# Transposing the rows of the experts and the logits by SyncE's DMAs in place of TensorE

## The reference

```python
xn = (xf - mu) * rsqrt(var + LN_EPS) * ln_scale + ln_bias
logits = xn @ gate_w.T                                   # 8 experts
tk_probs, tk_idx = top_k(softmax(logits), 2)
out = _swiglu(xf, sWg, sWu, sWd)                         # the shared expert, all rows
for e in range(NUM_EXPERTS):
    out = out + w[:, e:e + 1] * _swiglu(xf, Wg[e], Wu[e], Wd[e])
# _swiglu(x, wg, wu, wd) = silu(x @ wg) * (x @ wu) @ wd; 256 -> 512 -> 256
```

## Time and profile before

| what | us |
|---|---|
| median of 3 runs | 1809.16 |
| lowest and highest of the 3 | 1805.05, 1817.86 |
| the profiled execution | 1808.69 |
| its span, which the profile shows | 1807.0 |

### The profile page before, as it was taken

One profiled execution on the slowest core, in us unless ns is written; L12 is line 12 of the kernel. 1 busy time (PEld: TensorE's weight loads), 2 busy tenths in 40 slices (PEclk: granted clock), 3 DMA queues, 4 the chain that ended last, 5 costly groups with the idle time before them and its releaser, 6 DMA issues.

```text
span 1807.0 us, 44792 instructions
## 1 busy us (share of the span) xinstructions
PE 1611.0 (89%) x15824; PEld 1177.5 (65%) x15827; DVE 1105.0 (61%) x1938; ACT 881.9 (49%) x1305; POOL 888.4 (49%) x1125
## 2 busy tenths in 40 slices
PE   2589999999999999766987859979999999999996
PEld 2345555555555555356866737768999999999985
DVE  6568888888888888753764735653444444444432
ACT  1366676676666666543422325633444444444442
POOL 1145555555555555312034445625666666666652
PEclk9799999999999999986999979989999999999999
DMA  2323333333333333235366213222434334343432
GB/s 67 97 92 97 107 111 110 108 109 107 110 108 107 118 106 95 81 110 162 114 187 176 85 39 88 77 83 48 65 64 64 64 61 67 60 65 61 65 59 25
DMA packets 162574, 163.52 MB, mean 90 GB/s; under 512 B 23537, under 2 KB 153073, under 8 KB 162418
## 3 DMA queue, kind: packets, MB, share of 16 engines
q1 hardware_dynamic: 132210, 125.65, 22.7%
q0 software_dynamic: 30208, 35.81, 12.8%
HBM read 100.82 MB, written 60.30 MB: 89 GB/s over the span
## 4 chain that ended last, share of the span: by engine, by line
PE 67%; DMA 8%; issue 7%; DVE 6%; SPq 4%; ACT 3%; POOL 2%; another core or an unknown queue 2%; DVEq 0%; POOLq 0%; ACTq 0%
PE bank L1571 19%; PE pair_s L1861 13%; PE bank L1704 7%; PE pair_t L1861 6%; PE bank L1861 6%; PE pair_s L1631 4%; PE pair_t L1678 3%; PE bank L1739 3%; PE pair_t L1849 2%; SPq L435 2%; DMA wbuf<-in_L_ffn_Wu 2%; ACT prob L861 2%; DMA qk_d<-qkl 1%; DMA x_in<-xhl_d 1%
## 5 line engine op out<-in xcount | busy, mean ns | idle before, releaser
L861 ACT ACTIVATE prob<-pair_t 128x1024 f32<-128x1024 f32 x320 | 327.4, 1023 | 230.2 <-PE pair_t L1678 225.3
L665 POOL TENSOR_SCALAR_AFFINE_SELECT prob<-prob 128x256 f32<-128x256 f32 (+1 forms) x448 | 199.1, 458 | 324.6 <-ACT prob L861 320.2
L789 POOL DMA_INDIRECT out_x<-ysb,tok_rows x136 | 218.4, 1606 | 204.1 <-ACT ysb L1004 158.2
L968 ACT CAST early<-early 128x512 f16<-128x512 f32 (+1 forms) x208 | 125.1, 602 | 298.7 <-DVE early L1484 244.7
L1484 DVE SCALAR_TENSOR_TENSOR early<-pair_s,h_s,sg 128x512 f32<-128x512 f32 (+1 forms) x104 | 75.9, 729 | 243.6 <-PE pair_s L1861 209.6
L1490 DVE TENSOR_TENSOR early<-early 128x512 f16<-128x512 f32 (+1 forms) x208 | 139.2, 669 | 119.7 <-ACT early L968 86.7
L752 POOL DMA_INDIRECT tok_d<-tok_w,dest_i x128 | 130.3, 1018 | 157.6 <-PE bank L1861 69.0
L1861 PE MATMUL pair_s<-xt,wbuf 128*128 128x256 f16 (+1 forms) x1728 | 197.3, 270 | 4.5 <-DVE xt L1535 3.6
L1571 PE MATMUL bank<-wbuf,early 128*128 x1632 | 190.4, 273 | 0.9 <-ACT ysb L1004 0.8
L1704 PE MATMUL bank<-prob,v_op 128*32 128x512 f32 (+3 forms) x2048 | 181.2, 449 | 5.3 <-POOL prob L665 5.2
L1861 PEld LDWEIGHTS pair_s<-xt,wbuf 128*128 x1728 | 164.8, 99 | 26.6 <-issue 5.2
(11 more groups left out here) (261 smaller groups left out, 3051.9 us busy)
## 6 DMA issues: line engine op xcount, KB each, us to landing
q_op<-qk_d SPq DMA_DIRECT2D x192, 64.0 KB, 2.4
k_op<-qk_d SPq DMA_DIRECT2D x192, 64.0 KB, 2.4
x_in<-in_L_attn_x SPq DMA_DIRECT2D x16, 512.0 KB, 4.1
qk_d<-qkh SPq DMA_DIRECT2D x32, 256.0 KB, 2.2
qk_d<-qkl SPq DMA_DIRECT2D x32, 256.0 KB, 2.4
xres<-in_L_attn_x SPq DMA_DIRECT2D x16, 512.0 KB, 4.4
x_d<-x SPq DMA_DIRECT2D x32, 256.0 KB, 2.1
xhl_d<-xhl SPq DMA_DIRECT2D x32, 256.0 KB, 2.5
```

Of the source, the lines that this page charges most:

```text
L665: last = nc.gpsimd.affine_select(out=v, in_=v, compare_op=ALU.is_ge, fill=0.0, base=0, pattern=[[0, v.shape[1]], [1, P]], channel_multipli ...
L789: pool.indirect_dma_start(out=out, out_offset=bass.IndirectOffsetOnAxis(ap=tok_rows[:, k, 0:1], axis=0), in_=ysb[:, k % ROWS_AHEAD], in_of ...
L861: nc.scalar.activation(prob[:, half, u].rearrange("p a n -> p (a n)"), pair_t[:].rearrange("p a n -> p (a n)"), ACT.Exp, scale=exp_by).the ...
```

## The change

Every transpose of `xhl_d` rows, 8 (or 4) blocks of 128x128 per unit and 8 per logit pair, leaves PE, and with it the copy out of PSUM on ACT or VectorE. SyncE issues transposing DMAs (`dma_start_transpose`) instead, which write columns straight to SBUF:

- logits: one DMA of 512 rows per quad from DRAM, three buffers (two over `x_in`, one over `xn`) in place of two;
- shared expert: one DMA of 256 rows per unit from DRAM into `xts`, four buffers that lie over `xrow`; PE reads them there, and `xt2` is not used;
- routed stage: POOL gathers to `xrow` as before, and SP transposes each block, 128 rows, from `xrow` to `xt2`, SBUF to SBUF.

Waits follow: `columns(u)` waits for the hidden products of unit u-4, `gathered_columns` for those of unit u-2 and for the gather, PE for the transposes, `gather` for the transposes of the block eight before. The first four blocks' transposes stand in SP's program ahead of the last two stores of the shared stage.

```diff
-            def logit_rows(q):
-                if q < 2:
+            def logit_columns(q):
+                if q == 0:
                     sp.wait_ge(S["xn_done"], NB)
                     sp.wait_ge(S["stats_taken"], NB)
-                else:
-                    sp.wait_ge(S["lxT_in"], 2 * q - 2)
+                elif q == 2:
+                    sp.wait_ge(S["xnT_in"], 2 * NB)
+                elif q > 2:
+                    sp.wait_ge(S["lg_in"], 2 * (q - 3) + 2)
                 for j in range(2):
                     sp.wait_ge(xhl_stored[j], 16 * (q + 1))
-                sp.dma_start(lrow[:, q % 2], xhl_d[4 * P * q:4 * P * (q + 1), :].rearrange("(t p) n -> p t n", p=P)
-                             ).then_inc(lrow_loaded[q % 2], 16)
+                sp.dma_start_transpose(xtl[q % 3], xhl_d[4 * P * q:4 * P * (q + 1), :]).then_inc(xtl_loaded[q % 3], 16)
...
-            def rows(n):
-                if n >= GATHERED:
-                    sp.wait_ge(S["xT_in"], n - GATHERED + 1)
-                sp.dma_start(xrow[:, n % GATHERED], xhl_d[n * P:(n + 1) * P, :]
-                             ).then_inc(row_loaded[n % GATHERED], 16)
+            def columns(u):
+                if u >= 4:
+                    sp.wait_ge(S["u_in"], 2 * (u - 4) + 2)
+                sp.dma_start_transpose(xts[:, u % 4], xhl_d[2 * P * u:2 * P * (u + 1), :]).then_inc(xts_loaded[u % 4], 16)
...
+            def gathered_columns(k):
+                u, t = (k // 2, k % 2) if k < 2 * DBL else (k - DBL, 0)
+                if u > 1 and t == 0:
+                    sp.wait_ge(S["u_in"], 2 * (u + SH_UNITS - 2) + 2)
+                sp.wait_ge(row_gathered[k % GATHERED], 16 * (k // GATHERED) + 16)
+                sp.dma_start_transpose(xt2[:, u % 2, :, P * t:P * (t + 1)], xrow[:, k % GATHERED]
+                                       ).then_inc(xtr_loaded[u % 2], 16)
+
             for u in range(SH_UNITS):
+                if u == SH_UNITS - 1:
+                    for k in range(4):
+                        gathered_columns(k)
                 if u == LOADS_AT:
                     sp.wait_ge(S["lg_in"], TILES // 2)
+                if u + 4 < SH_UNITS:
+                    columns(u + 4)
                 for n in (2 * u, 2 * u + 1):
-                    if n + 6 < TILES:
-                        rows(n + 6)
                     store(n)
...
+            for k in range(4, BLOCKS):
+                gathered_columns(k)
...
             def gather(k):
-                pool.wait_ge(S["xT_in"], N_SH + k - GATHERED + 1)
+                if k < GATHERED:
+                    pool.wait_ge(S["u_in"], 2 * (SH_UNITS - 4 + k // 2) + 2)
+                else:
+                    done = k - GATHERED
+                    u = done // 2
+                    pool.wait_ge(xtr_loaded[u % 2], 32 * (u // 2) + 32)
...
             def routed(u, first, slot, turn, sizes):
                 par, (before, n, after) = slot_parity(u, slot), sizes
                 begin = at(offset[par])
+                pe.wait_ge(xtr_loaded[par], arrived(u, slot, turn))
                 for hh in range(2):
-                    unit_hidden(u + SH_UNITS, par, hh, P * n, begin)
+                    unit_hidden(u + SH_UNITS, xt2[:, par], hh, P * n, begin)
...
-                    unit_rows(u + (SH_UNITS + 1), row_gathered, [place_of(slot, turn, n + t) for t in range(after)])
```

More of the change, by code:

```diff
@@ L176, in build @@
         xhl = sb_a("xhl", [P, 2, 2, 2, C], F16)
-        lrow = x_in[:].rearrange("p a t c -> p (a t c)").bitcast(F16).rearrange("p (a t n) -> p a t n", a=2, t=4)
-        xtl = xn[:].rearrange("p t c -> p (t c)").bitcast(F16).rearrange("p (a t c n) -> p a t c n", a=2, t=2, c=2 * CC)
+        xtl = [x_in[:, k].rearrange("p t c -> p (t c)").bitcast(F16).rearrange("p (c n) -> p c n", c=2 * CC)
+               for k in range(2)]
+        xtl.append(xn[:].rearrange("p t c -> p (t c)").bitcast(F16).rearrange("p (c n) -> p c n", c=2 * CC))
         ctx_a.close()
@@ L194, in build @@
         spare = wbuf[:, (E - 1) * SLOT:]
[L195 to L197 removed]
+        xtl_end = spare[:, 0:2 * CC * 4 * P].rearrange("p (c n) -> p c n", c=2 * CC)
+        xts = xrow[:].rearrange("p g n -> p (g n)").rearrange("p (a c n) -> p a c n", a=4, c=2 * CC)
         zero_h = sb("zero_h", [P, 2 * C], F16)
@@ L239, in build @@
         ps_x16 = ps_x[:].bitcast(F16)
-        ps_lx = [bank[k][:].bitcast(F16) for k in (0, 1, 4, 6)]
         ps_r = bank[5]
@@ L336, in batches @@
             body(NB + 1, 1, cur=False, prev=False, prev2=True, nxt=False, nxt2=False)
-        row_loaded = [S[f"row_in{k}"] for k in range(GATHERED)]
+        xtr_loaded = [S[f"xtr_in{k}"] for k in range(2)]
+        xts_loaded = [S[f"xts_in{k}"] for k in range(4)]
         row_gathered = [S[f"rowg{k}"] for k in range(GATHERED)]
@@ L343, in build @@
         scattered = [S[f"scattered{k}"] for k in range(3)]
-        lrow_loaded = [S[f"lrow_in{k}"] for k in range(3)]
+        xtl_loaded = [S[f"lrow_in{k}"] for k in range(4)]
         N_SH = TILES
@@ L555, in load_matrix @@
                 sp.dma_start(dst.rearrange("p (c n) -> p c n", n=w.shape[2]), w).then_inc(S["w_exp"], 16)
-            for n in range(2):
-                rows(n)
-            sp.dma_start(lrow_end, xhl_d[NTOK - 4 * P:NTOK, :].rearrange("(t p) n -> p t n", p=P)
-                         ).then_inc(lrow_loaded[2], 16)
-            for n in range(2, 6):
-                rows(n)
+            columns(0)
+            sp.dma_start_transpose(xtl_end, xhl_d[NTOK - 4 * P:NTOK, :]).then_inc(xtl_loaded[3], 16)
+            for u in range(1, 4):
+                columns(u)
             for n in range(ROWS_AHEAD):
@@ L1543, in routed @@
                 unit_hidden(u + SH_UNITS, 1, P * n, 0)
-                if after:
-                    unit_rows(u + 1, 1 - par, first + (n + after), P * after)
                 unit_low(u + SH_UNITS, par, 1, P * n)
-            unit_rows(0, 0, 2, 2 * P)
             routed_units(dve, routed)
@@ L1789, in body, with logits @@
                         if k < PAIRS:
[L1790 to L1812 removed]
+                            logits(k, xtl[k // 2 % 3], xtl_loaded[k // 2 % 3], 16 * (k // 6) + 16)
+            def logits(k, columns, loaded, arrived):
+                pe.wait_ge(loaded, arrived)
                 if k == 0:
@@ L1839, in at, with hidden_half @@
                 return pe.snap(register, min_val=0, max_val=(E - 1) * SLOT)
-            def unit_rows(u, arrived, places):
-                for t, (here, count) in enumerate(places):
-                    pe.wait_ge(arrived[here], count)
-                    if t == 0 and some(u):
-                        pe.wait_ge(S["xt_done"], u)
-                    for c in range(2 * CC):
-                        to = P * (len(places) * c + t)
-                        last = nc.tensor.transpose(ps_x16[:, to:to + P], xrow[:, here, P * c:P * (c + 1)], ident_h[:])
-                    last.then_inc(S["xT_in"], 1)
-            def hidden_half(out, par, hh, w, begin, off):
+            def hidden_half(out, rows, hh, w, begin, off):
                 for k in range(2):
@@ L1860, in hidden_half @@
                             stationary = wsh[:, a:a + P] if begin is None else wbuf[:, bass.ds(begin + a, P)]
-                            last = nc.tensor.matmul(out[:, w * k:w * k + w], stationary, xt2[:, par, x, 0:w],
+                            last = nc.tensor.matmul(out[:, w * k:w * k + w], stationary, rows[:, x, 0:w],
                                                     start=(i == 0), stop=(i == 3 * CC - 1))
@@ L1934, in _ @@
             pe.reg_load(offset[0], unit_off[0:1, 0:1])
-            unit_rows(SH_UNITS, row_gathered, [place_of(0, 0, t) for t in range(2)])
             routed_units(pe, routed)
```

106 lines of the change are left out of this document (20 added, 86 removed).

## The result

The changed kernel takes 1745.07 us (median of 4 runs, 1741.02 to 1748.68) against 1809.37 us of the kernel before on the same chip: a ratio of 0.964, 95% interval 0.960 to 0.968. The profiled execution is 1744.72 us with a span of 1743.0 us. The forecast was 1746. The sum came out, but two of its terms did not: they missed in opposite directions, by about 10 us each.

A forecast was written before the change was run, and what follows sets the result against it. PE was taken to bound the routed stage; SP's load chain, VectorE, then PE to pace the shared stage. Terms -34 - 19 + 2 - 14 + 2 = -63 took 1808.7 to 1746 us; range 1726 to 1840, the forecast's own 1726 to 1785.

The forecast's parts named there:

- Routed stage, -34: Routed stage: PE loses its transposes, 0.50 us per double unit, 32 us plus 2 for single units, all on the path.
- The price of a transposing DMA: All transposing loads: taken at plain cost, 0.43 us of all engines for 128 KB; slow end 1.6 us per block.
- Drain, -19 and +2: Drain: first shared matmul at 830.4 instead of 849.72, -19 us; softmax shift loads behind three 512 KB loads, +2.
- issues behind waits in program order: Drain: the reason given for taking 2.5 us per logit load, nearer the best 1.7 than the worst 5.2.
- Shared stage, -14: Shared expert: -4 in units 0 to 4, -3 at the weight loads' end, -7 in the last 11 units.
- While the weights load, nothing: SP's chain paces it: Shared expert during weight loads: no gain beside the loads, only -3 us at the phase's end from rows fetched earlier.
- VectorE's phase: Shared expert after the weight loads, to 1059, paced by VectorE: no gain, since PE and ACT are not late there.
- Seam, +2: Shared to routed stage: +1 for a DMA of about 2.2 us, up to +1 for stores issued behind it.
- The rivals: Whole kernel: pieces at packet cost, 1810 us, chance 0.15; serialised transposes, about 2045, 0.16; routed unit not shortened, 1780, 0.05.
- logit loads over 6 us apart: Drain: a sign that the forecast is wrong; the rival with pieces at packet cost, chance 0.15, had 6.4 us.
- waits that name `xt<-xrow`: Routed stage: a sign that the forecast is wrong, if PE's waits there name this transfer.
- the routed unit did shorten: Routed stage: the rival said it doesn't, POOL's adds or DMA queues becoming the bound; 1780 us, chance 0.05.

The follow-up runs named there:

- `u_routed`: The changed kernel with the routed stage's part undone (transposes on PE and VectorE's copy back): 1730.32 us, ratio 0.979 to the kernel before.
- `twice`: The changed kernel with every gathered block from the fifth on transposed a second time, into a buffer nobody reads: 1707.03 us.
- `shift_first`: The changed kernel with its first three transposing logit loads issued after the load of the shifted rows: 1735.69 us, ratio 0.958 to the kernel before.
- all four of chip 14: The changed kernel run again unedited (1738.68 us, ratio 0.961 to the kernel before), `shift_first`, `plain_logits` and `pace`.
- `plain_logits`: The changed kernel with its drain logit loads as plain, untransposed copies of the same bytes, only the drain to be read: 1737.25 us, first shared product at 834.81.
- `ahead3`: The changed kernel with shared rows fetched three units ahead instead of four: 1711.3 us in one run.
- `u_shared`: The changed kernel with the shared expert's part undone (tile loads, PE transposes, ACT copies): 1728.59 us, ratio 0.977 to the kernel before.
- `pace`: The changed kernel with scatters after the 28th waiting for six more hidden products: 1723.72 us, ratio 0.953 to the kernel before.
- `best`: The changed kernel with logit loads behind the shifted rows' load, 36 tiles scattered ahead, token rows loaded a unit earlier: 1690.15 us, ratio 0.956 to the kernel before.

## Why the prediction was right, and where it was not

- **Routed stage, -34: right**, 31 measured from the second unit on, and the unit is 7.86 us (7.8 forecast) with PE at 100 % and no wait on `xt` but the 5.6 us of the first. Of the 0.50 us that the `LDWEIGHTS` rows gave for a unit's transposes, 0.45 were on the path. `u_routed` returns them.
- **The price of a transposing DMA: the step that was mis-sized.** The forecast took plain cost. Measured are 0.67 us of all engines for 128 KB (0.43 taken), 4.9 us median landing for 512 KB (4.2 taken, but plain loads at this pace land after 5.0), and a term that the sum did not have: 1.22 us of SyncE's own time for 128 KB, 2.2 to 2.4 for 512 KB. A 128x128 transpose by DMA takes 1309 ns by the Trainium skill, "VectorE: DVE Perf Modes", section "The three transpose paths". By that as a rate, `twice` would need 4 x 5.2 = 21 us in a unit, and it stays at 7.86: the trace disagrees with it as a rate. The rule of the Trainium skill, "Advanced Engine Details and Errata", section "X-Bar Transpose (TRN2)", that these DMAs are as fast as plain ones, agrees with the landings (4.9 and 5.0 us for 512 KB) and not with the rest: the engines' time is 1.6 times the plain figure, and the issuing queue is held 3 to 6 times as long as the 0.37 to 0.44 us of a plain issue.
- **Drain, -19 and +2: wrong, -5.9 measured.** The forecast had the fourth logit load out at 793.5, one every 2.5 us, and 4.2 us to land: last landing 825.2. The kernel before issued its fourth at 797.70; here it goes out at 802.20, for two reasons: the gate-scale product is 7.1 us late where I had put 2 as a term of its own, and the load stands in SyncE's program behind a half batch's stores (801.21), so it leaves 10.1 us behind that product in this kernel and in all four of chip 14, where I had 8.5. The twelve loads are 2.88 us apart (802.20 to 833.93), and the last is used at 838.72. That is +8.7, +4.2 and +0.6 us, and they make the 13.5 us between 830.4 and 843.9. The sentence that failed is that SyncE "issues behind waits in program order" and nothing more: an issue on it has a length. `shift_first` shows that this length, ahead of the shift load, is 6 of the 7.1 us (the last was there before the loads). The pace of 2.88 us is that of a queue that hardly stops; that the engines, loaded too, would not have held the same pace is not shown. `plain_logits` takes both away and gains 5.8 us (7.1 from the common store).
- **Shared stage, -14: wrong in its distribution, -24 measured.** "While the weights load, nothing: SP's chain paces it" failed: 13.8 us came there. The main cause is the look-ahead, which the forecast had priced at 3: one unit less costs 11 us in that phase on one chip (`ahead3`), 7 of which last to unit 19. VectorE's phase, forecast at nothing, gave 4.5; no run says why. Units 22 to 31 gained nothing here, although a unit's length fell as forecast where PE ran undisturbed (8.31 to 7.86 us, as `u_shared` and `u_routed` show on one chip). Short stalls stand there in its place (units of 9.3 to 12.5 us); they come beside GpSimd's scatters, but `pace` did not remove them, and their cause is open.
- **Seam, +2: right in size**, 1.9. The wait of 5.6 us for `xt` has behind it the token rows, which SyncE loads behind two stores; with that load earlier `best` waits 1.6. The 4.5 us that the first routed unit gained had no term.
- **The rivals** fell as said: no logit loads over 6 us apart, no waits that name `xt<-xrow` in the steady stage, and the routed unit did shorten.

Too much from the drain (11 us) and too little from the shared stage (10 us) made an agreement within 1 us of the total that is luck; the verdict, faster by over 1%, did not hang on either.

## What to carry to other kernels

Moving transposes from TensorE to DMA pays where TensorE never idles and the loads run ahead, at 0.45 us per unit here. Count such a DMA on its issuing engine, 1.2 to 2.4 us each, and put short loads that others wait for ahead of it: in the drain, without work to hide behind, most of the forecast gain was lost there. Look-ahead that the change brings along can be worth as much as the instructions it removes; read a chain that names one queue all along as "this queue is full", and ask what in it PE waits for. Before two executions are compared at a late mark, take a common mark just ahead of the edit: without it `shift_first` seemed worth 3 us and is worth 6.

## What was not expected of the hardware

- A transposing DMA holds SyncE: 1.22 us for 128 KB from SBUF, 1.24 for 256 KB and 2.4 for 512 KB from DRAM. At eight per unit of 10.6 us this is the bound, at a DMA share of 0.89.
- Pieces of 256 bytes cost about 0.021 us of one DMA engine each, less than half of the mean packet of the kernel before (0.050).
- TensorE's matmuls come one by one, with no wait on data, while GpSimd issues indirect DMAs without a pause; later issue of them returns 15 us on a chip with the hole. Two other chips show no hole in eight kernels, six of them with the same scatters, and the kernel before is 44 us faster there.
